# Second mixture of experts: mixing weights of four groups side by side, and the first item's mixed rows made a block earlier

## The chip, the cores and the metric

The kernel runs on one core of a Trainium2 chip. The metric is device time in microseconds (us), the median of the runs shown; a profiled execution of the same program gives the trace. The engines are TensorE (PE, with its weight loads as PEld), VectorE (DVE), ScalarE (ACT), GpSimd (POOL) and SyncE (SP), which issues most transfers.

## What is computed

Two transformer layers over 1024 tokens of 256 numbers. The part that matters here is the last one, a mixture of experts in the second layer (`T` = 1024 tokens, `F` = 8 groups, `K` = 8 places in each, inner width `I` = 176):

```python
scores = jax.nn.softmax(x @ gate_weight.T, axis=-1)
topk_w, topk_idx = jax.lax.top_k(scores, TOPK)
w_dense = jnp.zeros((T, E), x.dtype).at[jnp.arange(T)[:, None], topk_idx].add(topk_w)
flat = w_dense[:, inv_mapping]
scalar = flat.sum(-1)
soft = jax.nn.softmax(jnp.where(flat == 0, -1000000000.0, flat), axis=-1)

def expert(muW, gW, gqa, gqb, gs, uW, uqa, uqb, us, dW, dqa, dqb, ds, w):
    xe = x + w @ muW.T
    gate = jax.nn.silu(_fused_linear(xe, gW, gqa, gqb, gs, w))
    up = _fused_linear(xe, uW, uqa, uqb, us, w)
    return _fused_linear(gate * up, dW, dqa, dqb, ds, w)
outs = jax.vmap(expert, ...)(..., soft)
y = jnp.einsum('fth,tf->th', outs, scalar).reshape(b, s, h)
sh = jax.nn.silu(hidden_states @ sh_gate_W.T) * (hidden_states @ sh_up_W.T) @ sh_down_W.T
return y + sh
```

So each token has eight mixing weights `w` for each group, `xe` is the token plus a mix of the group's rows (the mixed rows), and `sh` are the shared experts. Products are made to float32 accuracy out of three passes: a high part and a low part of each operand, high times low, low times high, high times high.

## The kernel before

The program is a row of blocks; at the end of a block all engines meet before any starts the next. Three blocks matter. All line numbers are those of the profile.

**The gate's block** (to 435 us): the normalised tokens are turned (`hT`), split (`nhi`, `nlo`), and multiplied with the gate.

**The shared experts' block** (435 to 489 us) does two things at once. The shared experts run as four items `q` (two halves of the inner width, two halves of 512 tokens): `hidden(q)` on PE makes 18 matmuls into banks 4 to 6; ACT takes silu (`silu(q)`, lines 1961 and 1963), DVE multiplies (`hf`, line 1859), ACT rounds to the high part (`high(q)`, line 1968), DVE makes the low part (line 1863; both DVE steps are in `split(q)`), PE multiplies down (`down(q)`, 24 matmuls) and DVE adds to `x` (`accumulate(q)`, line 1873). Beside it the mixing weights are made from the gate's logits, in two halves of the tokens: DVE chooses the six largest (lines 1888 to 1901), PE turns and regroups them (`by_place`, lines 1814 and 1820), DVE and ACT take the softmax of each group (lines 1914 to 1942 and 1984), and the result `wst`, in three parts, is turned on PE (line 1839) and copied to `wT` (lines 1951 and 2000). ACT also makes the high part of group 0's weights (`high_part`, line 1637). POOL then makes their low part (`low_part`, line 1632) and signals `prep_ready`; on that SP loads group 1's weights into the same `raw`; POOL scales them (lines 1605 and 1608) and stacks the group's rows `mus` (lines 1615 to 1623). All of this is in the block, so the block can't end before POOL's last step.

**The groups' block** (489 us to the end): sixteen items `n`, eight groups by two halves of the tokens. For each PE makes the inner product `qa` (bank 2), the weights spread over 64 rows by `selw` (line 2138), the mixed rows of the next item (`mixed`, line 2115), the three streams, the outer products (line 2166) and the down products of the item before. DVE adds `hT` to the mixed rows (`xef`, line 2199), ACT rounds them (`xhi`, line 2273), DVE makes `xlo` (line 2203). Before item 0 the three engines make its mixed rows, with nothing beside them. Down products wait for `h1lo` (line 2235). `over_items` runs items 0 to 3 and 12 to 15 as straight code, and items 4 to 11 in a loop of two rounds on each engine, with waits against register values. SP and POOL loop over the groups too.

Each engine takes its instructions in the order in which they are written; what orders them across engines is waits on counts (semaphores) alone. `wT` stands on 32 partitions, group beside group along the free dimension, so that a turned bank, which holds four groups in its 128 partitions, is copied in four instructions.

## Time and profile before

| what | us |
|---|---|
| median of 3 runs | 718.03 |
| lowest and highest run | 717.14, 724.79 |
| profiled execution, its own time | 722.72 |
| its span, first to last instruction | 721.0 |
| PE busy, share of the span | 610.2 (85%) |
| DVE busy | 485.8 (67%) |
| ACT busy | 345.6 (48%) |
| POOL busy | 259.4 (36%) |

All times of the trace count from the start of the span. A row of the timeline gives start, length, engine, line, operation, output and inputs, and in brackets how long the engine had been idle before and what it waited for. PE's rows overlap, since matmuls are pipelined: their pace is the distance between starts. `PEq` or `POOLq` as the releaser is the meeting of the engines between blocks.

### The profile page before, as it was taken

The page shows a single profiled execution, that of the slowest core. Times are in us where ns is not written, and L with a number is a line of the kernel's source. Part 1 is how long each engine was busy: PE and PEld are TensorE (multiplying, and loading weights), DVE is VectorE, ACT ScalarE, POOL GpSimd, SP SyncE. Part 2 cuts the span into 40 slices and gives each one's busy share as a digit, 9 for nine tenths or more (in the row PEclk, how much of TensorE's full clock was granted, in tenths as well). Part 3 has the DMA queues.
Part 4 walks back from the last instruction along what each step waited for, and adds up shares of the span by engine and source line. Part 5 has one row for each costly group of instructions (what it writes and reads, how often), then busy time and mean ns, then how long its engine had stood idle before and what let it go on. Part 6 is the DMA issues. An engine that isn't in the chain of part 4 may idle for free. (4 is left out here: it accounts for less than half of the span.)

```text
span 721.0 us, 11966 instructions
## 1 busy us (share of the span) xinstructions
PE 610.2 (85%) x4144; PEld 482.7 (67%) x4144; DVE 485.8 (67%) x850; ACT 345.6 (48%) x605; POOL 259.4 (36%) x241
## 2 busy tenths in 40 slices
PE   3669868769999999994568658897899999999996
PEld 2357535669999999994324356674676776776775
DVE  4137274778777777750759979664778877878764
ACT  2324107257686867671167634445454454454431
POOL 4312120542343434343368713231443453453300
PEclk9859777989999999998679868988999999999998
DMA  8931262649677977722521020200202202202001
GB/s 272 277 97 32 67 213 79 242 175 314 207 227 203 262 198 223 209 30 30 189 59 44 15 87 1 75 8 0 83 1 82 82 2 81 81 0 82 0 1 58
DMA packets 59584, 79.12 MB, mean 110 GB/s; under 512 B 6720, under 2 KB 51728, under 8 KB 58512
## 3 DMA queue, kind: packets, MB, share of 16 engines
q1 hardware_dynamic: 53344, 71.09, 31.3%
q0 software_dynamic: 5088, 6.05, 4.8%
q10 hardware_dynamic: 1104, 1.35, 0.6%
q8 instruction: 29, 0.48, 0.3%
q14 instruction: 19, 0.16, 0.1%
HBM read 66.10 MB, written 12.37 MB: 109 GB/s over the span
## 5 line engine op out<-in xcount | busy, mean ns | idle before, releaser
L923 POOL DMA_INDIRECT moe_sum<-yb,xs x30 | 65.7, 2190 | 117.9 <-ACT yb L1067 80.8
L981 PE MATMUL bank<-xhi,wlo 128*128 128x256 f32 x240 | 69.7, 290 | 7.0 <-DVE xlo L1226 7.0
L1632 POOL TENSOR_TENSOR wlo<-raw,whi 128x1408 fp32r<-128x1408 f32 (+1 forms) x16 | 45.9, 2885 | 76.6 <-ACT whi L1637 76.6
L981 PE MATMUL bank<-xlo,whi 128*128 128x256 f32 x240 | 69.2, 289 | 0.0
L981 PE MATMUL bank<-xhi,whi 128*128 128x256 f32 x240 | 69.2, 288 | 0.0
L999 PE MATMUL bank<-whi,hlo 128*128 128x256 f32 x240 | 68.7, 286 | 0.0
L999 PE MATMUL bank<-whi,hhi 128*128 128x256 f32 x240 | 67.7, 282 | 0.0
L999 PE MATMUL bank<-wlo,hhi 128*128 128x256 f32 x240 | 67.6, 281 | 0.0
L2101 PE MATMUL bank<-xhi,wlo 128*128 128x512 f32 x128 | 54.4, 425 | 2.4 <-DVE xlo L2203 2.4
L1054 ACT ACTIVATE ga<-bank,b1s 128x256 f32<-128x256 f32 x120 | 49.7, 466 | 6.9 <-remote 2.9
L1235 DVE TENSOR_TENSOR hlo<-ga,hhi 128x512 fp32r<-128x512 f32 x60 | 39.8, 688 | 18.9 <-ACT hhi L1057 18.9
L981 PEld LDWEIGHTS bank<-xhi,wlo 128*128 128x128 f32 x240 | 47.2, 197 | 7.6 <-DVE xlo L1226 7.6
L2101 PE MATMUL bank<-xlo,whi 128*128 128x512 f32 x128 | 50.9, 397 | 0.0
L2101 PE MATMUL bank<-xhi,whi 128*128 128x512 f32 x128 | 50.7, 396 | 0.0
L981 PEld LDWEIGHTS bank<-xlo,whi 128*128 128x128 f32 x240 | 47.2, 197 | 0.0
L981 PEld LDWEIGHTS bank<-xhi,whi 128*128 128x128 f32 x240 | 47.2, 197 | 0.0
L999 PEld LDWEIGHTS bank<-wlo,hhi 128*128 128x128 f32 x240 | 45.4, 189 | 0.0
L999 PEld LDWEIGHTS bank<-whi,hlo 128*128 128x128 f32 x240 | 45.2, 188 | 0.0
L999 PEld LDWEIGHTS bank<-whi,hhi 128*128 128x128 f32 x240 | 45.1, 188 | 0.0
L156 POOL TENSOR_TENSOR kx<-ctxT,hmask 128x512 f32<-128x512 f32 x32 | 36.7, 1175 | 11.5 <-PE bank L1423 7.3
L1057 ACT ACTIVATE hhi<-ga 128x512 fp32r<-128x512 f32 x60 | 38.0, 633 | 1.9
L2213 DVE SCALAR_TENSOR_TENSOR x<-bank,scal,x 128x256 f32<-128x256 f32 x64 | 28.9, 482 | 12.7 <-PE bank L2101 11.9
(357 smaller groups left out, 1640.5 us busy)
## 6 DMA issues: line engine op xcount, KB each, us to landing
raw<-w_in SPq DMA_DIRECT2D x21, 1024.0 KB, 7.9
rawb<-w_in SPq DMA_DIRECT2D x14, 1024.0 KB
raw<-wf_in SPq DMA_DIRECT2D x8, 1088.0 KB
moe_rows<-zrow SPq DMA_DIRECT2D x2, 1935.0 KB, 17.3
xs<-moe_rows SPq DMA_DIRECT2D x15, 258.0 KB
scb<-sc_in SPq DMA_DIRECT2D x16, 160.0 KB
w2x<-w_in SPq DMA_DIRECT2D x2, 1024.0 KB, 8.2
cv<-ctx_in SPq DMA_DIRECT2D x32, 64.0 KB, 2.1
```

The costliest lines, as they stand in the source:

```text
L156: nc.gpsimd.tensor_tensor(kx[:, j, k, :, :], rows(keys, mask.shape[1]), each(mask, S), ALU.mult).then_inc(kx_ready, 1)
L923: nc.gpsimd.indirect_dma_start(xacc, bass.IndirectOffsetOnAxis(ap=xs[:, i % 4, t, D:D + 1].bitcast(I32), axis=0), yb[:, i % 2, t, :], None ...
L981: last = nc.tensor.matmul(psum[b][:, half:half + ST], w[:, s, at:at + P], a[:, s, k, :], start=(n == 0), stop=(n == 3 * KT - 1))
L999: last = nc.tensor.matmul(y_bank(i)[:, t * D:(t + 1) * D], h[:, s, m, t * P:(t + 1) * P], w[:, s, at:at + D], start=(n == 0), stop=(n == 3 ...
L1054: nc.scalar.activation(ga[:, b, cols], psum[b][:, cols], ACT.Gelu, bias=b1s[:, i % 4, m:m + 1]).then_inc(act_ready, 1)
L1057: nc.scalar.activation(hhi[:, s, 2 * b:2 * b + 2, :].rearrange("p m t -> p (m t)"), ga[:, b, :], ACT.Copy).then_inc(hi_ready, 1)
L1235: nc.vector.tensor_tensor(hlo[:, s, part, :].rearrange("p m t -> p (m t)"), ga[:, b, :], hhi[:, s, part, :].rearrange("p m t -> p (m t)"). ...
L1632: nc.gpsimd.tensor_tensor(wlo[:, s, a:b], raw[:, a:b], whi[:, s, a:b].bitcast(F32), ALU.subtract).then_inc(to, 1)
L2101: done = nc.tensor.matmul(bank, w[i], a[j], start=first and n == 0, stop=last and n == 3 * len(terms) - 1)
L2213: nc.vector.scalar_tensor_tensor(x[:, g, :], psum[DOWN_BANKS[t]][:, 0:D], scal[:, g, ds(col, 1)], x[:, g, :], ALU.mult, ALU.add).then_inc( ...
```

## The change

It has four parts, and nothing ahead of the gate's block is touched.

1. `wT` becomes 128 partitions by two: four groups lie side by side on the partitions, each in a place of 32. A turned bank is then copied by one instruction of 128 partitions. `mur`, `muh`, `mul`, `mus`, `selw` and `s1c` get 128 partitions, so that both operands of a group's matmul stand at the group's place.
2. The mixed rows of item 0 are made at the end of the shared experts' block, ahead of `down(3)` on PE and of `accumulate(3)` on DVE. The second slice goes to bank 4, once DVE has copied the weights out of it.
3. The orders in that block change: PE runs `hidden(1)` between the turning and the regrouping of the first half; `down(0)` waits for DVE's copy of the regrouped second half (`flat_ready`) and no longer for `z_ready`; DVE makes `hf` of item 0 ahead of choosing for the second half, and `split(2)` ahead of the second half's mixing weights; ACT does `silu(2)` and `high(2)` ahead of the high part of group 0's weights.
4. On PE, POOL and SP the loops over items and groups become straight code (on DVE and ACT they stay loops).

```diff
-            wT = buf("wT", [4 * K1, G1, T], F32R, s7)
+            wT = buf("wT", [P, G1 // 4, T], F32R, s7)
...
+            def place(g):
+                return slice(32 * (g % 4), 32 * (g % 4) + MS)
+
+            def mix_bank(i, k):
+
+                return psum[4] if i["n"] == 0 and k == 1 else psum[k]
+
+            def mixed(pe, i, k):
+
+                g = i["g"]
+                nc.tensor.matmul(mix_bank(i, k)[:, :], mus[place(g), i["s"], k * P:(k + 1) * P],
+                                 wT[place(g), g // 4, cols(i)], start=True, stop=True).then_inc(q8["mu_done"], 1)
...
                         hidden(0)
+                        turn(0)
+                        hidden(1)
                         by_place(0)
+                        turn(1)
                         by_place(1)
-                        hidden(1)
-                        pe.wait_ge(z_ready, 2)
+                        pe.wait_ge(flat_ready, 2)
                         down(0)
...
+                        pe.wait_ge(mus_ready, 1)
+                        for k in range(KT):
+                            pe.wait_ge(wT_ready, k + 1)
+                            mixed(pe, item_of(0, 0, 0), k)
                         down(3)
...
-                        split(0)
+                        choose(0)
+                        hidden_rows(0)
+                        choose(1)
+                        low_rows(0)
...
                         split(1)
                         accumulate(0)
+                        mixing_weights(0)
                         split(2)
+                        mixing_weights(1)
                         accumulate(1)
                         split(3)
                         accumulate(2)
                         dve.wait_ge(st_turned, 2)
-                        for g in range(4):
-                            nc.vector.tensor_copy(wT[:, g, CH:2 * CH],
-                                                  psum[ST_BANKS[1]][g * 4 * K1:(g + 1) * 4 * K1, :])
+                        dve.wait_ge(wT_ready, 1)
+                        nc.vector.tensor_copy(wT[:, 0, CH:2 * CH], psum[ST_BANKS[1]][:, :]).then_inc(wT_ready, 1)
+                        for k in range(KT):
+                            wait(dve, "mu_done", k + 1)
+                            mixed_sum(dve, item_of(0, 0, 0), k)
+                        for k in range(KT):
+                            wait(dve, "xhi_ready", k + 1)
+                            mixed_low(dve, item_of(0, 0, 0), k)
                         accumulate(3)
...
                         high(1)
+                        silu(2)
+                        high(2)
                         act.wait_ge(scaled_ready, 1)
                         high_part(0, 0)
                         high_part(0, 1)
...
-                        silu(2)
-                        high(2)
                         silu(3)
                         high(3)
-                        for n in (0, 2, 3):
-                            act.wait_ge(st_turned, n + 1)
-                            for g in range(4):
-                                nc.scalar.activation(wT[:, n // NCH * 4 + g, (n % NCH) * CH:(n % NCH + 1) * CH],
-                                                     psum[ST_BANKS[n]][g * 4 * K1:(g + 1) * 4 * K1, :], ACT.Copy)
+                        act.wait_ge(st_turned, 1)
+                        nc.scalar.activation(wT[:, 0, 0:CH], psum[ST_BANKS[0]][:, :], ACT.Copy).then_inc(wT_ready, 1)
+                        for k in range(KT):
+                            wait(act, "xef_ready", k + 1)
+                            mixed_high(act, item_of(0, 0, 0), k)
+                        for c in range(NCH):
+                            act.wait_ge(st_turned, NCH + c + 1)
+                            nc.scalar.activation(wT[:, 1, c * CH:(c + 1) * CH], psum[ST_BANKS[NCH + c]][:, :], ACT.Copy)
...
-                        mixed(item_of(0, 0, 0))
-                        over_items(pe, body)
+                        over_items(pe, body, unrolled=True)
...
-                        mix(item_of(0, 0, 0))
                         wait(dve, "zero_ready", 2)
...
-                        mix(item_of(0, 0, 0))
                         nc.scalar.preload_act_table(ACT.Silu)
```

How this moves instructions is seen best in the queues. ACT, in the shared experts' block, from the rounding of item 1 to the block's end (lines 1968: high parts of the multiplied rows, 1637 the weights' high parts, 1991 a part of the mixing weights, 2000 the copies to `wT`), before:

```order
L1968 ACTIVATE hhi<-hn 48x512
L1637 ACTIVATE whi<-raw 128x1408
L1637 ACTIVATE whi<-raw 128x768
L1991 ACTIVATE wst<-wst 128x32x8 x2
L1961 ACT_TABLE_LOAD
L1961 ACTIVATE hn<-bank 128x512
L1963 ACTIVATE hn<-bank 48x512
L1968 ACTIVATE hhi<-hn 128x512
...
L2000 ACTIVATE wT<-bank 32x512 x12
```

and the same place of the changed program (its lines 2032 and 2034 are silu, 2039 `high`, 1679 `high_part`, 2064 the mixing weights, 1628 `xhi`):

```order
L2032 ACT_TABLE_LOAD
L2032 ACTIVATE hn<-bank 128x512
L2034 ACTIVATE hn<-bank 48x512
L2039 ACTIVATE hhi<-hn 128x512
L2039 ACTIVATE hhi<-hn 48x512
L1679 ACTIVATE whi<-raw 128x1408
L1679 ACTIVATE whi<-raw 128x768
L2064 ACTIVATE wst<-wst 128x32x8 x2
...
L2069 ACTIVATE wT<-bank 128x512
L1628 ACTIVATE xhi<-xef 128x512 x2
L2075 ACTIVATE wT<-bank 128x512 x2
```

The silu of item 2 and its rounding now stand ahead of the weights' high parts and of the mixing weights, and twelve copies have become three, with item 0's `xhi` between them.

DVE at the end of the same block, in the changed program (1932 is `accumulate`, 2017 the copy to `wT`, 1624 `mixed_sum`, 1631 `mixed_low`); before, the row of line 2017 was four copies of 32 partitions and the two rows under it were the first of the next block:

```order
L1932 SCALAR_TENSOR_TENSOR x<-bank,tg,x 128x256 x4
L2017 CAST wT<-bank 128x512
L1624 TENSOR_TENSOR xef<-bank,hT 128x512 x2
L1631 TENSOR_TENSOR xlo<-xef,xhi 128x512 x2
L1932 SCALAR_TENSOR_TENSOR x<-bank,tg,x 128x256 x4
L1801 UNCONDITIONAL_BRANCH
```

Item 0's sums and low parts moved over the block's end (the branch in the last row) to ahead of the last accumulation.

PE at the place of the regrouping, in the changed program (1857 turning, 1822 the shared experts' matmuls, 1866 regrouping; of the eighteen matmuls of `hidden(1)` the first and the last stand here); before, both turnings and both regroupings stood together, ahead of `hidden(1)`:

```order
L1857 MATMUL bank<-ident,pre 64x128 x4
L1822 MATMUL bank<-nhi,wlo 128x512
...
L1822 MATMUL bank<-nhi,whi 128x512
L1866 MATMUL bank<-sel,wdT 128x64 x4
L1857 MATMUL bank<-ident,pre 64x128 x4
L1866 MATMUL bank<-sel,wdT 128x64 x4
L1822 MATMUL bank<-whi,hlo 128x256
```

Eighteen matmuls moved ahead of three short steps; `down(0)` (the last row) now follows the second regrouping directly.

## Rows read from the trace of the kernel before

**Rows 1.** Chain that ended last, in order of time: start, us, what.

```profile
489.23 0.78 PE bank L2115
```

**Rows 2.** Timeline of PE: where each step of these blocks starts.

```profile
440.21 0.63 PE L1814 MATMUL bank<-ident,pre 128*64 128x128 f32 x4 [0.32 <-DVE pre L1901]
...
446.28 0.79 PE L1779 MATMUL bank<-nhi,wlo 128*128 128x512 f32 x1
...
452.98 0.28 PE L1779 MATMUL bank<-whi,hlo 128*128 128x256 f32 x1
...
457.27 0.50 PE L1779 MATMUL bank<-nhi,wlo 128*128 128x512 f32 x1
...
461.58 0.28 PE L1779 MATMUL bank<-whi,hlo 128*128 128x256 f32 x1
...
469.70 0.77 PE L1779 MATMUL bank<-nhi,wlo 128*128 128x512 f32 x1 [3.76 <-DVE hn L1859]
...
476.59 0.28 PE L1779 MATMUL bank<-whi,hlo 128*128 128x256 f32 x1
...
480.89 1.97 PE L1839 MATMUL bank<-ident,wst 128*128 128x128 f32 x16
482.61 0.37 PE L1779 MATMUL bank<-whi,hlo 128*128 128x256 f32 x1
...
489.23 1.19 PE L2115 MATMUL bank<-wT,mus 24*128 24x512 f32 x2 [2.20 <-PEq L1758]
492.86 0.76 PE L2101 MATMUL bank<-xhi,wlo 128*128 128x512 f32 x1 [2.44 <-DVE xlo L2203]
```

**Rows 3.** Stretches: us, busy of each engine, granted TensorE clock, DMA share, GB/s.

```profile
473.00:475.00 2.00, 2.00 (x7) 1.54 (x6) 0.00 (x0) 0.29 (x1) 1.71 (x3) 0.50 0.00 0
493.00:495.00 2.00, 2.00 (x5) 1.61 (x6) 0.00 (x0) 0.29 (x1) 0.00 (x0) 0.50 0.00 0
```

**Rows 4.** Timeline of ACT, shared experts' block.

```profile
456.76 2.10 ACT L1637 ACTIVATE whi<-raw 128x1408 fp32r<-128x1408 f32 x2
463.65 0.42 ACT L1991 ACTIVATE wst<-wst 128x256 fp32r<-128x256 f32 x1 [4.80 <-DVE wst L1940]
...
466.05 1.28 ACT L1961 ACT_TABLE_LOAD   x1
...
481.58 7.21 ACT L2000 ACTIVATE wT<-bank 32x512 fp32r<-32x512 f32 x12 [2.76 <-PE bank L1839]
```

**Rows 5.** Timeline of DVE: regrouped halves, then the mixing weights.

```profile
446.36 0.42 DVE L1914 COPY big<-bank 128x256 f32<-128x256 f32 x1
...
448.87 0.42 DVE L1914 COPY big<-bank 128x256 f32<-128x256 f32 x1
...
460.08 1.70 DVE L1936 TENSOR_TENSOR big<-big,tg 128x256 f32<-128x256 f32 x1
461.82 1.80 DVE L1940 CAST wst<-big 128x256 fp32r<-128x256 f32 x1
...
464.83 0.42 DVE L1936 TENSOR_TENSOR big<-big,tg 128x256 f32<-128x256 f32 x1
465.29 0.29 DVE L1940 CAST wst<-big 128x256 fp32r<-128x256 f32 x1
```

**Rows 6.** Timeline of POOL: low parts of group 0; last step of group 1.

```profile
458.27 5.20 POOL L1632 TENSOR_TENSOR wlo<-raw,whi 128x1408 fp32r<-128x1408 f32 x2 [16.53 <-ACT whi L1637]
...
476.08 0.73 POOL L1623 TENSOR_TENSOR mus<-mul 24x256 fp32r<-24x256 f32 x1
```

**Rows 7.** Timeline, groups' block: DVE's low part, PE's products behind it, twice.

```profile
596.99 0.69 DVE L2235 TENSOR_TENSOR h1lo<-h1f,h1hi 64x512 fp32r<-64x512 f32 x1 [0.69 <-ACT h1hi L2304]
597.88 0.39 PE L2101 MATMUL bank<-whi,h0lo 128*128 128x256 f32 x1 [0.50 <-issue]
...
678.19 0.69 DVE L2235 TENSOR_TENSOR h1lo<-h1f,h1hi 64x512 fp32r<-64x512 f32 x1 [0.69 <-ACT h1hi L2304]
678.98 0.36 PE L2101 MATMUL bank<-whi,h0lo 128*128 128x256 f32 x1 [0.21 <-issue]
```

More of the change, by code:

```diff
@@ new lines, in wait, with item_of, cols @@
+            def wait(engine, name, value):
+                if not isinstance(value, int) or value > 0:
+                    engine.wait_ge(q8[name], value)
+            def item_of(g, s, c):
+                return dict(g=g, s=s, c=c, n=g * NCH + c)
+            def cols(i):
+                return slice(i["c"] * CH, (i["c"] + 1) * CH)
+            def place(g):
+                return slice(32 * (g % 4), 32 * (g % 4) + MS)
+            def mix_bank(i, k):
+                return psum[4] if i["n"] == 0 and k == 1 else psum[k]
@@ L2064, in _ @@
                     def _(sp):
-                        with sp.Fori(2, G1) as g:
+                        for g in range(2, G1):
                             sp.wait_ge(prep_ready, g)
@@ L2083, in _ @@
                             low_part(pool, 1, 1, part)
-                        with pool.Fori(1, G1 // 2) as it:
+                        for it in range(1, G1 // 2):
                             for s in range(2):
@@ L2107, in weights @@
                             return whi[r, s, a:b], wlo[r, s, a:b]
-                        def mixed(i):
-                            pe.wait_ge(mus_ready, i["g"] + 1)
-                            wait(pe, "xef_ready", KT * i["n"])
-                            apart(pe, turns)
-                            for k in range(KT):
-                                nc.tensor.matmul(psum[k][:, :], mus[:, i["s"], k * P:(k + 1) * P],
-                                                 wT[0:MS, ds(i["g"], 1), cols(i)].rearrange("r o t -> r (o t)"),
-                                                 start=True, stop=True).then_inc(q8["mu_done"], 1)
                         def stream(i, j, src):
@@ L2137, in body @@
                                 apart(pe, turns)
[L2138 to L2140 removed]
+                                nc.tensor.matmul(psum[3][:, :], selw[place(i["g"]), :],
+                                                 wT[place(i["g"]), i["g"] // 4, cols(i)], start=True, stop=True).then_inc(q8["we_done"], 1)
                             if nxt is not None:
[L2142 removed]
+                                pe.wait_ge(mus_ready, nxt["g"] + 1)
+                                wait(pe, "xef_ready", KT * nxt["n"])
+                                apart(pe, turns)
+                                for k in range(KT):
+                                    mixed(pe, nxt, k)
                             if i is not None:
```

118 lines of the change are left out of this document (63 added, 55 removed).

## The prediction

> **What bounds the kernel now.** I read first the chain that ended last. From 489 us on nearly all of it is PE's matmuls; what isn't is short, and the longest stretch without PE lies at the start of the groups' block: the mixed rows of item 0 leave at 489.23 [rows 1], and the first product that uses them starts at 492.86, after PE has waited 2.44 for DVE's `xlo` [rows 2]. So 3.6 us there are latency (PE, DVE, ACT, DVE in turn). Then I read PE's timeline through the shared experts' block. PE is the engine that ends this block's products, with these holes: 3.76 us ahead of `hidden(3)` at 469.70, waiting for DVE's `hf` of item 2, and 2.20 us at the block's end, where the other engines finish [rows 2]. ACT is the last of those: its twelve copies to `wT` run from 481.58 for 7.21 us, to 488.79 [rows 4], 0.44 us before PE goes on. The hole at 469.70 has a cause in the queues: ACT stood waiting for the mixing weights 4.80 us ahead of line 1991, and only after both parts of them did it load the silu table at 466.05 [rows 4]; item 2's products had been ready since 461.58 [rows 2]. Third, the clock. At 473 to 475 and at 493 to 495 us the granted clock is 0.50, the 1.2 GHz level [rows 3], after these holes: 18 matmuls of `hidden` take 4.31 us at 457.27 to 461.58 and 6.89 us at 469.70 to 476.59 [rows 2]. Each long hole costs its own length and some 2.5 us more.
>
> **The shared experts' block, followed queue by queue.** I lay the new orders out with the rows' durations; start 435.5 and the first choice stay. (a) DVE makes `hf` of item 0 straight after the first choice (440.2 [rows 2], two steps of 0.7), so `hidden(1)` runs 441.5 to 445.8 at the full clock instead of 446.28 to 452.98, where it took 6.7 [rows 2]. That gives nothing by itself: the regrouping of the second half now comes behind it and ends near 448.5, ACT rounds item 0 only after both copies of the turned weights, DVE's low rows end near 449.7, the first half's steps take 2.5 (446.36 to 448.87 [rows 5]), and the copy for which `down(0)` waits ends near 452.7. Before, `down(0)` started at 452.98 [rows 2]. PE stands some 4 us instead. If the clock falls in that hole as it did after 3.76 us at 469.70, `down(0)` takes about 1.4 us more than its 4.3 (24 matmuls, each some 0.06 longer; an estimate, bounds 0 and 2.5, the loss of `hidden(3)`). (b) `hidden(2)` then ends at 461.2, or 462.6 with the slow clock. Its silu no longer waits for the mixing weights: table load 1.28, silu, DVE's `hf`, and that is ready at 462.6 (464.0), before `down(1)` ends at 465.5 (466.9). So `hidden(3)` starts there and runs at the full clock to 469.8 (471.2) instead of 476.59: the hole of 3.76 and the 2.6 of slow clock go, 6.8 us (5.4 with the loss in (a)). (c) `down(2)` 4.3 more, turning 1.7 (480.89 to 482.61 [rows 2]): 475.8 (477.2). The copy of bank 0 takes 0.6, an instruction over 128 partitions taking no more than one over 32 (7.21 for twelve [rows 4]), DVE's copy of bank 4 behind it 0.7; PE's two mixed products follow, with a wait of some 0.3 us that `down(3)` now stands behind, and `down(3)` ends at 480.7 (482.1). Item 0's sums, high and low parts (2.6 us) go under these 4.3 us, DVE's last accumulation is at 481.2 (482.6), ACT's last copies end before that. The work that hides them is `down(3)`; without it they would cost their 3.6.
>
> **POOL sets the block's end instead.** ACT makes the high parts of group 0 only after `high(2)`, at 463.3 (464.7) and not at 456.76 [rows 4]. From that start, low parts by POOL (5.20), SP's load of group 1, scaling and stacking took until 476.81 [rows 6]: 20.05 us, as a chain that nothing else in the block shortens. It now ends at 483.3 (484.8), about 2 us after PE and DVE. With the 0.44 of the meeting, item 0's first product starts at 483.8 (485.2) instead of 492.86. I take 484.5, between them: **8.4 us gained** (bounds 7.6 and 9.1).
>
> **Item 0's clock.** PE again stands, some 3 us, before that product. Before, about eight matmuls ran at the slow level (0.19 each: 1.5 us), after `hidden(3)`'s hole thirteen did (2.5). I take 0.8 us lost; bounds are 1.5 gained, if the clock doesn't fall, and 1.1 lost.
>
> **Items 4 to 11 as straight code on PE.** DVE's `h1lo` ends at 597.68 and PE goes on at 597.88, 0.20 later, in the loop; in the straight items it ends at 678.88 and PE goes on at 678.98, 0.10 later [rows 7]. The 0.10 are gone in eight items: 0.8 us gained. Bounds: nothing, if DVE and ACT, still loops, set the pace, and 1.6, if a second wait in an item gains too. Straight code on POOL and SP lies beside PE's work: the loads are issued an item ahead of need. If that cover were gone an item would wait for it, but each saves time rather than takes it. The Trainium skill (Runtime: NRT & Kernel Launch, Instruction fetch mechanics) says that a taken branch out of the fetched window stalls the engine, so that straight code should be worth more. No hole stands on PE where the loop goes back (between 597.88 and the next down products only their own wait is idle), so the trace doesn't bear out a price, and the sum has none.
>
> **Contention, which speaks against the change.** POOL's low parts ran 458.27 to 463.47 [rows 6]; in it two DVE steps took 1.70 and 1.80 that take 0.42 and 0.29 beside an idle POOL [rows 5]: 2.8 us. They now run at about 464.7 to 470, beside the second half's mixing weights and ahead of `accumulate(1)`, for which `down(2)` waits at 469.8. With 2.8 us on them the first accumulation ends near 469.1, so 0.7 us are left there, and PE has 2 us more before it would pass POOL's end. The Trainium skill (SBUF — State Buffer, Who interferes with whom) says that a DVE step with two inputs in SBUF is blocked by a GpSimd step that reads it until that one ends. By this a third step could lose up to the 3.3 us of one low part, and the end would move by nothing to 0.6; the rows agree with the kind of step.
>
> **Sum.** −8.4 + 0.8 − 0.8 = −8.4 us. The profiled execution was 722.72 in all (span 721.0); it would become 714.3. The median of the runs is 4.7 lower, and the steps don't depend on that: 718.03 − 8.4 = **709.6 us**.
>
> **Rivals.** (1) As above, 0.60: 706.5 to 712.5. (2) The moved splitting costs more: POOL's chain starts behind item 2, and each delay of DVE or PE before it (a slow `down(0)` with a slow `hidden(2)`, 2.5 + 2.6, or a blocked `hf`) moves the block's end one for one. For it speaks that this chain has no slack, against it that the slow clock at 469.70 cost no more than 2.6 in all. With 3 to 5 us more: 713 to 715, 0.20. (3) Half the block's gain is lost again in item 1, whose down products wait on a chain through ACT and DVE: that chain starts from PE's own products, which move along, so I give it 0.06: about 714. (4) More than the sum, since neither hole costs clock: 1.5 + 1.4 + 0.8 on top, below 706.5: 0.09. (5) Slower: PE's straight code in items 4 to 11 is starved by its instruction stream. Each of the eight would need more than 8.4/8 = 1.05 us of hole; at 2 us each, the longest hole of PE near here (2.44), 709.6 + 16 = 726. Nothing in items 12 to 15, straight already, shows one: 0.05.
>
> **How the numbers follow.** The likeliest case gives 709.6. The range takes in rivals (1) and most of (2) and (3): 706.5 to 714.5. One per cent, about what a measurement of this kernel can tell from no change, is 7.2 us: 710.85. Of (1) somewhat over three quarters lies below it, with (4) 0.57 faster; the rest of (1), (2) and (3) 0.38 the same; (5) 0.05 slower.
>
> **What would show it.** In the changed profile: `hidden(1)` starts near 441.5 and a hole of some 4 us stands before `down(0)`; no hole before `hidden(3)`, which runs at 2.4 GHz; ACT's `whi` starts at 463 to 465; POOL's last `mus` of group 1 ends last in the block, near 484; item 0's first product is at 484 to 485.5; PE goes on 0.1 after `h1lo` in items 4 to 11 too. The forecast is wrong if the first product is later than 487, if `hidden(2)` or `down(2)` waits for DVE, or if holes that the trace puts on nothing appear among items 4 to 11.

## The result and the profile after

The changed kernel is slower. Its median is 727.26 us (four runs, 726.53 to 727.28) beside 717.59 for the kernel before on the same chip: a ratio of 1.0116, 95% interval 1.0070 to 1.0161 (the two medians alone give 1.0135, inside it). The forecast was 709.6.

The blocks ahead of the shared experts' block are the same instructions in both, but their length differs from execution to execution: the first shared product starts at 435.46 in the trace of before, at 431.07 in that of the changed kernel, and between 426.57 and 433.77 in the traces of the experiments. So everything below is counted from that product. Three stretches are used throughout: **A**, from the first shared product to the first product of item 0; **B**, from there to the first down product of item 1; **C**, from there to the end of the span. Each is a difference of starts in PE's timeline.

| kernel | A | B | C | A+B | in all |
|---|---|---|---|---|---|
| before | 57.40 | 22.39 | 205.75 | 79.79 | 285.54 |
| before, second execution | 55.51 | 25.33 | 205.71 | 80.84 | 286.55 |
| changed | 61.19 | 25.31 | 206.63 | 86.50 | 293.13 |
| forecast (484.5 − 435.46; +0.8; −0.8) | 49.0 | 23.2 | 205.0 | 72.2 | 277.2 |

The two executions of before differ in A and in B by 2 to 3 us and in A+B by 1.05: the granted clock may fall a little earlier or later, and what one stretch wins the other loses. A+B is the steadier measure, good to about 1 us. The changed kernel loses 5.7 to 6.7 us there and 0.9 in C, together 6.6 to 7.6, which is what the medians show (1.16% of 717.59 is 8.3, with an interval of 5.0 to 11.6).

PE's timeline of the changed kernel: start, length, operation, in brackets the idle time before and what it waited for. It answers to [rows 2].

```profile
431.07 0.47 PE L1822 MATMUL bank<-nhi,wlo 128*128 128x512 f32 x1 [0.85 <-PEq L1709]
...
437.22 0.47 PE L1822 MATMUL bank<-nhi,wlo 128*128 128x512 f32 x1 [0.78 <-DVE hn L1909]
...
448.73 0.58 PE L1822 MATMUL bank<-whi,hlo 128*128 128x256 f32 x1 [3.70 <-DVE big L1976]
...
456.22 0.79 PE L1822 MATMUL bank<-nhi,wlo 128*128 128x512 f32 x1
...
462.58 0.28 PE L1822 MATMUL bank<-whi,hlo 128*128 128x256 f32 x1
...
466.85 0.50 PE L1822 MATMUL bank<-nhi,wlo 128*128 128x512 f32 x1
...
472.71 0.36 PE L1822 MATMUL bank<-whi,hlo 128*128 128x256 f32 x1 [1.40 <-DVE x L1932]
...
482.56 1.22 PE L1619 MATMUL bank<-wT,mus 24*128 24x512 f32 x2
483.71 0.58 PE L1822 MATMUL bank<-whi,hlo 128*128 128x256 f32 x1
...
492.26 0.77 PE L2162 MATMUL bank<-xhi,wlo 128*128 128x512 f32 x1 [0.99 <-PEq L1801]
```

In order these are the starts of `hidden(0)`, `hidden(1)`, `down(0)`, `hidden(2)`, `down(1)`, `hidden(3)`, `down(2)`, the mixed rows, `down(3)` and item 0. `hidden(3)` has no hole before it any more, as intended. But a new one of 1.40 us stands before `down(2)`, and then everything is slow: `down(2)`, the turning and the mixed rows take 11.0 us (472.71 to 483.71), where `down(2)` and the turning of before took 6.0 (476.59 to 482.61 in [rows 2]), and `down(3)` runs for 7.5 instead of 4.3. The granted clock in stretches (busy time of PE, PEld, DVE, ACT, POOL, then the clock, DMA share, GB/s), which answers to [rows 3]:

```profile
452.00:458.00 6.00, 6.00 (x19) 4.59 (x19) 4.46 (x10) 0.73 (x2) 0.00 (x0) 0.50 0.00 0
...
462.00:470.00 8.00, 8.00 (x42) 6.22 (x41) 6.41 (x8) 4.05 (x6) 3.77 (x2) 1.00 0.00 0
...
480.00:486.00 6.00, 6.00 (x23) 4.57 (x22) 3.21 (x6) 2.48 (x5) 3.74 (x6) 0.50 0.00 0
...
500.00:504.00 4.00, 4.00 (x18) 2.86 (x16) 1.29 (x2) 0.66 (x2) 0.00 (x0) 0.78 0.00 0
```

There are two slow stretches at 1.2 GHz: from 447.1 to 460.7, beginning within the hole of 3.70, and from 474.4 to 501.7, behind the hole of 1.40. The second lasts 27 us, though PE stands only once more in it, for 0.99 us at the block's end. What runs in it until 492 is thin, matmuls of 256 columns and turnings of 128, but for the two of the mixed rows.

Who was late for `down(2)`: DVE's timeline, then ACT's and POOL's, which answer to [rows 5, 4, 6].

```profile
466.28 3.45 DVE L1997 TENSOR_TENSOR big<-big,tg 128x256 f32<-128x256 f32 x1
469.77 1.82 DVE L2001 CAST wst<-big 128x256 fp32r<-128x256 f32 x1
471.62 0.42 DVE L2003 TENSOR_TENSOR wst<-big,wst 128x256 fp32r<-128x256 f32 x1
472.08 1.66 DVE L1932 SCALAR_TENSOR_TENSOR x<-bank,tg,x 128x256 f32<-128x256 f32 x4
```

```profile
443.28 0.59 ACT L2049 ACTIVATE wdT<-bank 64x512 f32<-64x512 f32 x1 [6.21 <-PE bank L1857]
443.78 1.14 ACT L2039 ACTIVATE hhi<-hn 128x512 fp32r<-128x512 f32 x2
...
464.72 2.10 ACT L1679 ACTIVATE whi<-raw 128x1408 fp32r<-128x1408 f32 x2
```

```profile
466.23 5.21 POOL L1674 TENSOR_TENSOR wlo<-raw,whi 128x1408 fp32r<-128x1408 f32 x2 [28.89 <-ACT whi L1679]
...
483.64 0.72 POOL L1665 TENSOR_TENSOR mus<-mul 24x256 fp32r<-24x256 f32 x1
```

POOL starts its low parts at 466.23 and DVE its division of the second half's mixing weights at 466.28. DVE's step takes 3.45 us and the one behind it 1.82, where 0.42 and 0.29 are enough beside an idle POOL [rows 5]. So `accumulate(1)` starts at 472.08, and `down(2)`, whose `hidden(3)` has been done since 471.3, waits for it. POOL itself, which the forecast had as the last engine of the block, is done at 484.36, 7.9 us before item 0.

In the groups' block the same pair of engines meets once more. Of [rows 7] the answer is, in POOL's, DVE's and PE's timelines of two successive items in the middle of the block:

```profile
590.15 3.26 POOL L1674 TENSOR_TENSOR wlo<-raw,whi 128x1408 fp32r<-128x1408 f32 x1 [7.24 <-ACT whi L1679]
...
590.25 3.71 DVE L2312 TENSOR_TENSOR h1lo<-h1f,h1hi 48x512 fp32r<-48x512 f32 x1
...
600.47 0.69 DVE L2287 TENSOR_TENSOR h1lo<-h1f,h1hi 64x512 fp32r<-64x512 f32 x1 [0.69 <-ACT h1hi L2354]
...
601.25 0.36 PE L2162 MATMUL bank<-whi,h0lo 128*128 128x256 f32 x1 [2.00 <-issue]
```

POOL began the low part of a group's weights at 590.15, and DVE's `h1lo`, otherwise 0.68, took 3.71; DVE then ran late through the item, and at the next down products PE stood 2.00 us. PE does go on 0.09 after `h1lo` (601.16 to 601.25), as straight code was expected to.

### The profile page after: what moved, and what is told of

Its sections match the earlier page's. It is cut to its first block and busy times, and to the rows that moved or that the text cites. A ratio compares the mean times of both kernels' runs of the same rounds, so it can differ in the third digit from the quotient of the medians.

```text
span 724.2 us, 11760 instructions
## 1 busy us (share of the span) xinstructions
PE 616.0 (85%) x4144; PEld 489.0 (68%) x4144; DVE 486.0 (67%) x847; ACT 339.1 (47%) x596; POOL 260.2 (36%) x241
## 5 line engine op out<-in xcount | busy, mean ns | idle before, releaser
L1235 DVE TENSOR_TENSOR hlo<-ga,hhi 128x512 fp32r<-128x512 f32 x60 | 39.7, 687 | 17.5 <-ACT hhi L1057 16.5
L1054 ACT ACTIVATE ga<-bank,b1s 128x256 f32<-128x256 f32 x120 | 49.5, 465 | 2.6 <-PE bank L981 0.9
L156 POOL TENSOR_TENSOR kx<-ctxT,hmask 128x512 f32<-128x512 f32 x32 | 36.6, 1173 | 11.5 <-PE bank L1423 7.4
```

The lines of the kernel that those rows point to most:

```text
L156: nc.gpsimd.tensor_tensor(kx[:, j, k, :, :], rows(keys, mask.shape[1]), each(mask, S), ALU.mult).then_inc(kx_ready, 1)
L1054: nc.scalar.activation(ga[:, b, cols], psum[b][:, cols], ACT.Gelu, bias=b1s[:, i % 4, m:m + 1]).then_inc(act_ready, 1)
L1235: nc.vector.tensor_tensor(hlo[:, s, part, :].rearrange("p m t -> p (m t)"), ga[:, b, :], hhi[:, s, part, :].rearrange("p m t -> p (m t)"). ...
```

## The experiments

Twelve more kernels ran, the first of them the kernel before once more. The theory: the loss comes from one place. ACT's `high_part(0)` stands behind `high(2)`, so POOL's low parts fall on DVE's second half of the mixing weights, and the short hole before `down(2)` lets the clock fall with only thin matmuls to follow. The rivals: the moved mixed rows, the early `hidden(1)`, or the straight code cost the time. Ratios are to the kernel before on the same chip.

| run | median | ratio, 95% interval | A | B | C | A+B |
|---|---|---|---|---|---|---|
| changed | 727.26 | 1.0116 [1.0070, 1.0161] | 61.19 | 25.31 | 206.63 | 86.50 |
| b1_pe_straight | 716.18 | 0.9945 [0.9897, 0.9993] | 57.17 | 22.33 | 205.50 | 79.50 |
| b2_all_straight | 720.18 | 1.0037 [0.9988, 1.0085] | 57.31 | 22.33 | 205.39 | 79.64 |
| e1_whi_early | 712.90 | 0.9906 [0.9871, 0.9941] | 52.58 | 21.01 | 206.39 | 73.59 |
| e2_pool_later | 720.94 | 1.0034 [0.9990, 1.0079] | 56.47 | 24.86 | 206.29 | 81.33 |
| e3_filler | 719.67 | 1.0015 [0.9968, 1.0063] | 55.96 | 24.76 | 206.18 | 80.72 |
| e4_high0_early | 708.89 | 0.9875 [0.9834, 0.9915] | 48.66 | 21.02 | 207.81 | 69.68 |
| e5_pool_behind_hlo | 712.68 | 0.9949 [0.9910, 0.9988] | 52.80 | 21.01 | 206.40 | 73.81 |
| e6_mixed_back | 719.64 | 1.0051 [1.0006, 1.0097] | 54.60 | 25.05 | 207.68 | 79.65 |
| e7_old_first_items | 711.62 | 0.9864 [0.9818, 0.9911] | 46.98 | 22.38 | 206.55 | 69.36 |
| e8_interleaved | 707.66 | 0.9829 [0.9742, 0.9915] | 46.31 | 21.02 | 207.40 | 67.33 |
| e9_third_last | 706.95 | 0.9874 [0.9804, 0.9943] | 43.37 | 21.01 | 207.67 | 64.38 |

### The kernel before, once more

> The kernel before, unchanged, for a second profile. The one on record took 722.7 us, 5 us above the median of its runs, and reached the gate's block some 4.4 us later than the changed kernel did, with the same instructions up to there. If that is only the spread of the stages before, this profile has the gate's and the shared experts' blocks with the same lengths as the first (57.4 us from the first shared product to the first product of item 0) and is shorter ahead of them, in all about 717 to 718.

A 55.51, B 25.33, C 205.71 (the second row of the first table); its own time was 715.34. The blocks ahead were shorter, as expected, but A wasn't 57.4 again: the same instructions took 1.9 us less there and B 2.9 more. So the comparison of traces has to start at the first shared product, and A and B go together.

### Straight code alone

On the kernel before, the loop of PE alone as straight code:

```diff
-                        over_items(pe, body)
+                        over_items(pe, body, unrolled=True)
```

> The kernel before, with PE's items 4 to 11 as straight code and nothing else. Prediction on record: 0.8 us faster, bounds 0 and 1.6: about 717. Rival (the instruction stream of straight code starves PE, or new phases between DVE and POOL cost a hole of 2 us as at 599 to 601 us in the changed kernel): 719 to 726.

C became 205.50, 0.21 to 0.25 less than before. The sign was right and the size a third of the 0.8 forecast. The ratio of 0.9945 is some 4 us, far more than these stretches show, and the next run has the same code on PE and 1.0037; so it isn't put down to the code. Then POOL's and SP's loops too:

```diff
-                        with sp.Fori(2, G1) as g:
+                        for g in range(2, G1):
...
-                        with pool.Fori(1, G1 // 2) as it:
+                        for it in range(1, G1 // 2):
```

> The kernel before with the loops of PE, POOL and SP as straight code, the fourth part of the change alone. Theory A (POOL's weights come a little earlier without its loop, and meet DVE's low parts of items 4 to 11, which gives the hole of 2.00 us at 601 us of the changed kernel): from the down products of item 1 to the end 206.3 us or more instead of 205.75, and a hole of 1.5 to 2.5 us at one item in the middle of the groups' block. Theory B (that hole comes from the time at which POOL starts the block, not from its code): 205.2 to 205.8 us and no such hole; ratio to the kernel before 0.995 to 1.002 either way.

C is 205.39, in the range of theory B, and in the middle of the block no item waits longer than 0.44 us. The ratio of 1.0037 has 1 in its interval. The fourth part of the change alone neither starves PE nor gives a gain that the ratios could show. But theory B's own reason, the time at which POOL enters the groups' block, doesn't hold either: in e6 below POOL enters it 3.38 us ahead of item 0's first product (before: 3.81, changed: 0.19), and a hole of 1.97 stands at the same item. The hole is in every kernel that has the whole changed groups' block; what in it brings the hole (the new places of the weights and rows, with the straight code or without) was not tested.

### The weights' high parts early on ACT

The changed kernel, with `high_part(0)` and the mixing weights' part again ahead of silu and rounding of item 2:

```diff
-                        silu(2)
-                        high(2)
                         act.wait_ge(scaled_ready, 1)
                         high_part(0, 0)
                         high_part(0, 1)
...
+                        silu(2)
+                        high(2)
```

> The changed kernel, but ACT makes the high parts of group 0 ahead of silu(2), as before; silu(2) stays ahead of the mixing weights. Theory (contention, then the clock): POOL's low parts then fall on 454 to 460 and no longer on the second half's mixing weights; accumulate(1) is in time, the hole of 1.40 before down(2) goes, and the clock stays at 2.4 GHz from hidden(2) on until the block's end. Gain over the changed kernel: 1.4 + 2.0 (down(2)) + 1.9 (turning) + 3.2 (down(3)) + about 2 (item 0) = 10 us, so about 717. Rival (the clock falls since down, turning and the mixed products are thin, whatever the hole): 725 to 727. Rival (POOL's place doesn't matter, straight code on PE costs it): 727.

A+B fell from 86.50 to 73.59, 12.9 us where 10 were expected, and the ratio is 0.9906: this one exchange turns the change from a loss into a gain. POOL's and DVE's timelines, and PE's at `down(2)` and item 0:

```profile
453.09 4.96 POOL L1674 TENSOR_TENSOR wlo<-raw,whi 128x1408 fp32r<-128x1408 f32 x2 [16.89 <-ACT whi L1679]
```

```profile
465.33 1.00 DVE L1997 TENSOR_TENSOR big<-big,tg 128x256 f32<-128x256 f32 x1
466.37 0.72 DVE L2001 CAST wst<-big 128x256 fp32r<-128x256 f32 x1
...
467.81 1.66 DVE L1932 SCALAR_TENSOR_TENSOR x<-bank,tg,x 128x256 f32<-128x256 f32 x4
```

```profile
470.20 0.28 PE L1822 MATMUL bank<-whi,hlo 128*128 128x256 f32 x1
...
482.50 0.47 PE L2162 MATMUL bank<-xhi,wlo 128*128 128x512 f32 x1 [0.99 <-PEq L1801]
```

POOL is done with its low parts at 458.05, 7 us before DVE divides the second half (the 1.00 and 0.72 fall beside POOL's short scaling). `accumulate(1)` starts 2.4 us before `down(2)` is due, no hole stands there, and `down(2)` to item 0 takes 12.3 us instead of the 19.6 of the changed kernel.

### POOL later, and PE kept busy

The exchange of e1 moves two things: POOL's steps and ACT's. Two kernels change only one link each. In the first POOL waits until both halves of the mixing weights are made:

```diff
+                                pool.wait_ge(st_ready, 2 * NCH)
```

> The changed kernel, but POOL starts the low parts of group 0 only once the mixing weights of both halves are made (a wait for st_ready). Nothing is earlier; one collision is gone. Theory (contention, then the clock): DVE's two steps of 3.45 and 1.82 are 0.42 and 0.29 again, the hole of 1.40 before down(2) goes and with it the slow clock; POOL's chain ends some 2 us later, at about 486, and now ends the block; about 719 to 720. Rival (thin work lowers the clock, not the hole): no change, 726 to 728. If POOL's lateness counted, it would be slower than the changed kernel, 729.

```profile
488.35 0.77 PE L2163 MATMUL bank<-xhi,wlo 128*128 128x512 f32 x1 [4.49 <-PEq L1801]
```

The hole before `down(2)` is gone and the clock is 1.00 from 462.8 to 486.6. Now POOL ends the block, 55.8 us after the first shared product, and PE waits 4.49 us for it. Still A+B is 5.2 us shorter than in the changed kernel. In the second the contention stays, and only PE's hole is filled, with eight matmuls whose result nobody uses:

```diff
+                        for n in range(8):
+                            nc.tensor.matmul(psum[0][:, :], whi[:, 0, WN:WN + P], nhi[:, 0, 0:CH], start=True, stop=True)
                         down(2)
```

> The changed kernel, with eight matmuls of 512 columns more on PE between hidden(3) and down(2), into bank 0, whose contents nobody reads then. Eight take 8 x 0.23 = 1.9 us; the hole there is 1.4 to 1.8 us, so they fill it and add nearly nothing. Theory (it is the hole that lets the clock fall): from down(2) to the first product of item 0 the clock stays at 2.4 GHz, the stretch from down(2) to that product takes 14 to 15 us and not 19.6, item 0 runs at full clock too; about 8 us faster than the changed kernel, 719. Rival (the thin matmuls of down, turning and the mixed products let the clock fall by themselves): still slow from about 475 on, 727 to 728.

```profile
470.00:472.00 2.00, 2.00 (x11) 1.55 (x9) 1.93 (x6) 1.38 (x3) 0.00 (x0) 1.00 0.51 91
472.00:482.00 10.00, 10.00 (x60) 7.78 (x60) 8.86 (x17) 4.06 (x7) 3.56 (x5) 1.00 0.36 130
```

```profile
485.36 0.77 PE L2164 MATMUL bank<-xhi,wlo 128*128 128x512 f32 x1 [2.48 <-PEq L1801]
```

In these stretches (columns as above) PE runs the filler and then all the thin work at 2.4 GHz: the same matmuls, ready no sooner than before, and A+B is 5.8 us shorter. What PE did in 1.40 us decided over the clock of all the rest of the block. Item 0's clock, which was expected to hold as well, did not: here, too, POOL ends the block, as the forecast had it (but at 55.3 us, not at 48 to 49, since `high_part(0)` starts later), PE waits 2.48 for it, and around that wait the clock falls once more. So of the 12.9 us that e1 gives back some 6 are the clock behind the hole. Of the other 7, 1.9 are the hole itself, which e3 fills and doesn't remove (`down(2)` starts 42.2 us after the first shared product in e3, 40.3 in e1), and the rest hangs on POOL's chain, which was next in line: 1.5 of longer wait, and 3.8 in B, where the clock is at 0.50 from 483.4 to 493.7 in e3 and at 1.00 throughout in e1.

### The mixed rows back in the groups' block

The kernel of e1, with item 0's mixed rows, sums and low parts again at the start of the groups' block (the steps of PE, DVE and ACT moved over the meeting of the engines, in the old order):

```diff
-                        pe.wait_ge(mus_ready, 1)
-                        for k in range(KT):
-                            pe.wait_ge(wT_ready, k + 1)
-                            mixed(pe, item_of(0, 0, 0), k)
                         down(3)
...
+                        pe.wait_ge(mus_ready, 1)
+                        for k in range(KT):
+                            mixed(pe, item_of(0, 0, 0), k)
```

> e1_whi_early, with item 0's mixed rows back at the start of the groups' block; the copies to wT stay as in the change. On record: the latency of 3.6 us comes back, less what down(3) waited for them (0.3 to 1). If PE's long wait before item 0 also lets the clock fall, 1.5 us more in item 0. From the first shared product to the first product of item 0: 52.6 + 3 = 55.6; in all 3 to 5 us above e1. Rival: moving them gave nothing, since down(3) waited as long: equal to e1.

```profile
481.17 0.77 PE L2149 MATMUL bank<-xhi,wlo 128*128 128x512 f32 x1 [2.64 <-DVE xlo L1631]
```

```profile
480.00:490.00 10.00, 8.83 (x19) 6.15 (x20) 4.61 (x8) 4.03 (x6) 0.00 (x0) 0.50 0.00 0
```

The wait of 2.64 is back, and behind it 10 us at 1.2 GHz. A+B is 79.65 instead of 73.59: the move is worth 6.1 us, of which 2.0 are in A (the latency) and 4.0 in B (the clock of item 0, which with a wait of only 0.99 stays at 1.00 in e1). The rival that the moved mixed rows cost time falls. C is 1.3 us longer as well, and the two ratios are 1.45% apart, about 10 us; what is above 6.1 of it has no cause shown.

### The hole before down(0)

The kernel of e1, with the rounding of item 0 between ACT's two copies of the turned weights rather than behind them:

```diff
                         for c in range(NCH):
                             act.wait_ge(wd_turned, c + 1)
...
+                            if c == 0:
+                                high(0)
-                        high(0)
```

> e1_whi_early, and ACT rounds item 0 (high(0)) between its two copies of the turned weights rather than behind both. Theory: the hole of 3.70 before down(0) is DVE, waiting 4.3 for ACT's rounding, which stands behind the second copy. DVE is then free for the regrouped halves as they come; down(0) starts some 3 us earlier, the hole is 0.5 to 1 us, and the slow clock of down(0) and hidden(2), which cost 3.2 + 1.9, goes. From the first shared product to the first product of item 0: 52.6 in e1, here 45 to 47. About 705 to 707. Rival (another engine takes over, DVE or POOL): 48 to 52.

```profile
442.56 0.39 PE L1822 MATMUL bank<-whi,hlo 128*128 128x256 f32 x1 [0.68 <-DVE big L1976]
```

```profile
444.00:453.00 9.00, 9.00 (x27) 6.89 (x26) 8.25 (x14) 4.59 (x6) 4.93 (x2) 0.50 0.00 1
```

The hole shrinks from 3.70 to 0.68 us and A by 3.9, but 45 to 47 was expected and it is 48.66, in the rival's range and not for the rival's reason: the clock falls all the same, from 443.9 on, behind a hole of 0.68. So the length of a hole isn't all that decides. The trace of the kernel before had shown it. Beside the rows at 440.21 and 446.28 [rows 2] stand these two of the second half:

```profile
443.23 0.63 PE L1814 MATMUL bank<-ident,pre 128*64 128x128 f32 x4 [0.61 <-DVE pre L1901]
444.54 1.81 PE L1820 MATMUL bank<-sel,wdT 64*128 64x64 f32 x8 [0.68 <-ACT wdT L1978]
```

No hole there is longer than 0.68, and the granted clock is at 0.50 from 444.7 to 451.5, through most of `hidden(1)`. The question became what decides, and three orders were tried around this place. First PE and DVE as before the change (both turnings and regroupings, then `hidden(1)`; on DVE both choices first), with only ACT's order of e1:

```diff
                         turn(0)
-                        hidden(1)
                         by_place(0)
                         turn(1)
                         by_place(1)
+                        hidden(1)
...
                         choose(0)
-                        hidden_rows(0)
                         choose(1)
+                        hidden_rows(0)
```

> The changed kernel with ACT's silu(2) and high(2) early (run e1_whi_early), and the order of PE and DVE around the first two items as before: hidden(1) behind both regroupings, DVE's hidden rows behind both choices. Theory of the prediction (moving hidden(1) ahead only moved a hole of 4 us to ahead of down(0) and slowed its thin matmuls): without the move no hole stands before down(0), it takes 4.3 us instead of 7.3, and the stretch from the first shared product to the first product of item 0 is 49.5 to 51.5 us instead of 52.58, with a new hole of up to 4 us ahead of hidden(1). Rival (the move pays by giving DVE the regrouped logits earlier): 53.5 us or more, since the mixing weights, the weights' low parts and accumulate(1) come later and the hole before down(2) is back.

```profile
442.46 1.97 PE L1866 MATMUL bank<-sel,wdT 64*128 64x64 f32 x8 [0.68 <-ACT wdT L2049]
444.35 0.79 PE L1822 MATMUL bank<-nhi,wlo 128*128 128x512 f32 x1
...
450.88 0.28 PE L1822 MATMUL bank<-whi,hlo 128*128 128x256 f32 x1
```

A is 46.98, below the range of its own theory (49.5 to 51.5) and 5.6 less than in e1: the early `hidden(1)`, with ACT rounding item 0 as late as the change has it, was a loss by itself. The clock falls here too, at 442.4, but it meets 512-column matmuls: it is back at 2.4 GHz by 449.3, before the thin `down(0)`, which takes 4.3 us. Then, on the kernel of e4, `hidden(1)` early again, with its third product cut off and put between the thin steps (the new argument of `hidden` is the range of its products):

```diff
-                        hidden(1)
+                        hidden(1, range(0, 2))
                         by_place(0)
                         turn(1)
+                        hidden(1, range(2, 3))
                         by_place(1)
```

> The kernel with silu(2), high(2) and high(0) of ACT early (run e4_high0_early), and on PE hidden(1) cut in two: two of its three products, regrouping of the first half, turning of the second, the third product, regrouping of the second half. Theory (thin work in one stretch, turning and regrouping with the gap before down(0), is what lets the granted clock fall at 443): broken up by full matmuls the clock holds 1.00 through down(0), down(0) takes about 4.4 us instead of 7, and from the first shared product to the first product of item 0 it is 45 to 46.5 us instead of 48.66. Rival (the clock falls at the thin matmuls wherever they stand): the granted clock still falls to 0.50 at some point of down(0), and that stretch stays 48 to 49.5 us.

```profile
447.48 0.38 PE L1822 MATMUL bank<-whi,hlo 128*128 128x256 f32 x1 [0.52 <-DVE big L1977]
```

A is 46.31, in the theory's range, but its reason failed: the clock still fell, at 450.4, in the middle of `down(0)`, and stayed at 0.50 until 457.2. Last, both turnings ahead of both regroupings, and the third product behind them, directly before `down(0)`:

```diff
-                        by_place(0)
                         turn(1)
-                        hidden(1, range(2, 3))
+                        by_place(0)
                         by_place(1)
+                        hidden(1, range(2, 3))
                         pe.wait_ge(flat_ready, 2)
```

> Run e8_interleaved with one more exchange on PE: turning of the second half and both regroupings in one row, and the third product of hidden(1) behind them, right ahead of down(0). Theory (what precedes down(0)'s thin matmuls decides whether they meet a fall of the granted clock; a full product just before them keeps it, as full products kept it in run e7_old_first_items): down(0) takes 4.3 to 4.6 us at a granted clock of 1.00, though a hole of up to 0.7 us stays before it, and from the first shared product to the first product of item 0 it is 43 to 45 us. Rival (the thin stretch and its holes let the clock fall a few us later whatever follows at once): the fall still comes at about 16 us behind the first shared product, and the stretch stays 46 to 47 us.

```profile
447.14 0.39 PE L1822 MATMUL bank<-whi,hlo 128*128 128x256 f32 x1 [0.54 <-DVE big L1977]
```

```profile
447.00:452.00 5.00, 4.86 (x26) 3.77 (x27) 4.77 (x12) 4.36 (x7) 0.00 (x0) 1.00 0.00 2
452.00:461.00 9.00, 9.00 (x46) 7.00 (x45) 8.79 (x13) 5.29 (x8) 5.20 (x2) 1.00 0.22 75
```

The hole of 0.54 is as long as in e8 (0.52), and the same steps run; but with a full product ahead of it the clock doesn't fall at all up to the block's end. `down(0)` takes 4.4 us, A is 43.37, and A+B 64.38, 15.4 us less than before and 22.1 less than the changed kernel. The expectation (43 to 45, with the clock at 1.00) was met in both parts. It rests on one trace of each kernel, though, and the two executions of the kernel before show that the clock falls at other places from one execution to the next. The four runs of e8 lie between 701.46 and 711.86, its fastest ahead of all four of e9 (704.66 to 707.94). So that the place of the full product is the cause is likely and not shown; e9 moved the turning too.

### POOL out of DVE's way

The kernel of e1, with POOL's first low part of each group behind DVE's `hlo` of the item before, so that the two don't start together:

```diff
+                                    if part == 0:
+                                        wait(pool, "hlo_ready", 2 * (g - 1) * NCH + 2)
```

> e1_whi_early, and POOL, before the first low part of a group, waits until DVE has made the low part of h1 of the item before it. Theory: the hole of 2.00 in the middle of the groups' block is POOL starting its low part 0.1 us ahead of DVE's h1lo, which then takes 3.71 and not 0.68. With the order fixed the hole is 0.5 like the others: 1.5 us less in the stretch from item 1's down products to the end (206.4 in e1; here 204.5 to 205). Rival: the collision moves to another step of DVE, 206.

The hole of 2.00 became 1.28, most others grew by some 0.3 (0.45 to 0.74, 0.69 to 0.98, 0.75 to 1.05), and C stayed (206.39 in e1, 206.40 here): the rival was right, nothing is won by moving the meeting of the two engines within an item.

C differs by up to 1.6 us among the kernels that have the changed groups' block (206.18 to 207.81). About 1 us of it lies at the tail: from the last but three down products to the end it is 41.2 in e1, where the clock is at 0.50 for some 4 us behind the same two holes of 1.77 and 2.21 us, and 42.3 in e4, e8 and e9, where it is for some 7. No experiment was made on that.

## Why the prediction was wrong, step by step

**Contention was mis-sized, and that opened the hole.** The step "With 2.8 us on them the first accumulation ends near 469.1, so 0.7 us are left there" took the price from where the two engines had met before. There DVE's first step began 1.81 us into POOL's first instruction, with 1.5 of it left; here it began 0.05 us into it, and DVE lost 4.56 us (3.45 + 1.82 − 0.42 − 0.29). By the forecast's own timetable that is 1.1 us past the slack; measured, the hole is 1.40. The text had named the rule of the Trainium skill (SBUF — State Buffer, Who interferes with whom), that DVE's step is blocked until POOL's ends, and allowed a third step up to 3.3 us for it; the first step lost 3.0 (3.45 − 0.42), so by that rule the trace agrees. The cast behind it has one input only and lost 1.5 as well, which the text's "the rows agree with the kind of step" passes over. The error that counted was the next clause, "the end would move by nothing to 0.6": a hole of 1.1 was within the 2 us that PE had before it would pass POOL's end, so even with the right contention the sum would have stayed.

**The price of a hole was its length, and that decided.** The forecast charged the clock only behind holes of 3 to 4 us, and a hole before `down(2)` had no term for it. In the changed kernel the 1.40 us were followed by 27 us of slow clock. With the hole filled (e3) the same work up to the block's end ran at 2.4 GHz and A+B was some 6 us shorter. The sign was in the rows: the forecast quotes the 6.7 us of `hidden(1)` before and doesn't ask why; the holes ahead of it are of 0.68 and less.

**The clock's price on thin work was too low.** (a) gave `down(0)` 0.06 us more for each matmul, 1.4 in all, bounds 0 and 2.5. It took 7.5 instead of 4.3: 3.2 more, outside the bounds, 0.31 us for each matmul instead of 0.18. The slow clock also ran on through `hidden(2)`, which took 6.4 instead of 4.3. The hole itself (3.70, "some 4") and the start of `down(0)` (17.7 us after the first shared product, 17.5 before) were right.

**(b) was right in kind.** No hole before `hidden(3)`, which ran at 2.4 GHz. It started 35.8 us after the first shared product, where the forecast's case with a slow `down(0)` has 31.4 (466.9 − 435.5); the 1.8 and 2.1 of slow clock that it lacked make 35.3, and 0.5 are left over.

**(c) was right in kind and hidden by the clock.** The mixed rows did move under `down(3)`, and they are worth 6.1 us (e6 against e1), more than their latency of 3.6, since item 0's clock holds too. In the changed kernel the part that is clock is missing, since item 0 ran at 1.2 GHz there too.

**POOL sets the block's end: wrong here, right in e2 and e3.** Its chain took 19.6 us from ACT's start (464.72 to 484.36; 20.05 forecast), but the slow products ended later: PE's last 6.9 us after it and DVE's last accumulation 7.4. With the clock held (e3), POOL was last. So the two faults of the late `high_part(0)` stood behind each other, and taking away the first alone would have given the gain back only in part: A+B 80.7, no gain over the kernel before.

**Item 0's clock** cost 2.9 us in B (25.31 against 22.39), 0.8 forecast, bound 1.1: the same fault, since the clock was already low when item 0 started. The second execution of the kernel before has 25.33 in B, though, so this term by itself is no larger than what two executions of one kernel differ by.

**Straight code** gave 0.2 (b1) instead of 0.8: PE's wait behind `h1lo` is 0.1 shorter, but that is not what paces every item. The rule of the Trainium skill (Runtime: NRT & Kernel Launch, Instruction fetch mechanics) that a taken branch out of the fetched window stalls the engine isn't borne out here by more than that 0.2 in all of C. Rival (5), slower since PE is starved, the only one on the right side, was right in sign and wrong in mechanism: b2 has the straight code without its cost. Rival (2), a slow `down(0)` with a slow `hidden(2)`, saw that part of the mechanism, but priced it at 3 to 5 us and had POOL as the engine that passes it on.

In figures: A came out 12.2 us over the forecast, B 2.1 and C 1.7, 16.0 of the 17.7 between 709.6 and 727.26. Against the forecast's later case (item 0 at 485.2, so A 49.7) A is 11.5 over: 4.4 up to `hidden(3)`, and 7.1 behind it, where the hole and its clock lie. C's 1.7 are the 0.8 that the straight code was to give and 0.9 lost against the kernel before; the one new thing seen there is the hole of 2.00 in the middle, and its cause stays open. The forecast had named what would show it wrong, a late first product and a `down(2)` that waits for DVE; both came.

## What to carry to other kernels

An engine step that is moved takes its contention with it: before a POOL step with a long read of SBUF is moved, look what DVE does at the new time, and reckon with the whole length of the POOL instruction, not with what DVE lost at the old place. Price a hole on PE by what follows it: before thin matmuls a hole of 1.40 us cost several. To set a full-width product directly ahead of thin work is worth trying (e9, one trace, with a hole of 0.54 between them); with 1.40 between them the clock fell all the same. Mend the engine that is next in line (here POOL) in the same edit. The change was a good one with one order wrong: with ACT's two lines as before it is 0.94% faster, and with ACT's rounding of item 0 earlier and PE's products in e9's order too 1.3% (e9, interval 0.6 to 2.0%); by ratio e8 and e9 can't be told apart, by A+B e9 is 2.95 us shorter.

## What the runs showed of the hardware

A hole of 0.54 us between 512-column products and 256-column matmuls left the granted clock at 1.00 (e9), one of 1.40 between the same was followed by a fall to 0.50 (the changed kernel), and so were holes of 0.52 and 0.68 between regroupings of 64 columns and 256-column matmuls (e8, e4) and of 0.61 and 0.68 amid turnings and regroupings (the kernel before). Each is read from one execution, and from one execution to the next the falls move: in the kernel before the fall at `hidden(1)` came 9.3 and 10.4 us after the first shared product and lasted 6.8 and 3.4. In the changed kernel the clock then stayed at 0.50 for 18 us of mostly thin matmuls during which PE counted as busy all the time but for 0.99 us, and came back only after 9 us of item 0's products. At 0.50 a thin matmul of `down` takes 0.31 us and at 1.00 0.18, a factor of 1.7; one of 512 columns 0.43 and 0.23 to 0.24, a factor of 1.8.

DVE's `h1lo`, 0.68 alone, took 3.71 when it started 0.10 us after POOL's step, and the division of 0.42 took 3.45 when it started 0.05 after: POOL's instruction takes 3.26 (128x1408), and both DVE steps ended 0.2 to 0.6 us behind it. In the kernel before the same division began 1.81 into such an instruction and took 1.70 [rows 5, 6]: what a step loses is what is left of POOL's instruction when it begins.
